# A gated transformer block on one core: attention output turned by whole transposes into two banks, six gate banks for the last batch, operands filled with zeros, new step lists

## What is computed

```python
x = x + tanh(g_xattn[0]) * L0_xattn(ln(x), ctx)   # auto-correlation attention by FFT, top 5 delays
x = x + tanh(g_ffn[0])   * L0_ffn(ln(x))          # product keys: 8 heads x 8 of 1024 experts
x = x + tanh(g_xattn[1]) * L1_xattn(ln(x), ctx)   # 16 heads of 8 channels, rotary positions
x = x + tanh(g_ffn[1])   * L1_ffn(ln(x))          # 8 experts of 336 hidden units, silu(gate) * up
```

## Time and profile before

| what | us |
|---|---|
| median of three runs (lowest, highest) | 447.41 (446.62, 448.52) |
| profiled execution, its own time | 448.5 |
| its span, first to last instruction | 446.6 |
| TensorE busy | 375.3 (84%) |
| VectorE busy | 324.0 (73%) |
| ScalarE busy | 197.5 (44%) |
| GpSimd busy | 103.6 (23%) |

### The profile page before, as it was taken

How to read it: one execution, slowest core, us unless ns; L and a number is a source line. 1 busy time by engine, 2 the same in 40 slices (tenths; PEclk the granted TensorE clock), 3 DMA queues, 4 the chain that set the end, 5 groups by cost and what they waited for, 6 DMA issues and landing times.

```text
span 446.6 us, 8078 instructions
## 1 busy us (share of the span) xinstructions
PE 375.3 (84%) x2848; PEld 291.4 (65%) x2848; DVE 324.0 (73%) x1255; ACT 197.5 (44%) x399; POOL 103.6 (23%) x221
## 2 busy tenths in 40 slices
...
GB/s 232 332 240 0 1 1 1 1 48 118 1 1 0 1 1 0 1 2 2 0 2 1 1 3 0 1 2 1 13 1 0 1 3 12 1 0 1 13 0 12
DMA packets 5773, 11.81 MB, mean 26 GB/s; under 512 B 2020, under 2 KB 4325, under 8 KB 5222
## 3 DMA queue, kind: packets, MB, share of 16 engines
...
...
## 4 chain that ended last, share of the span: by engine, by line
PE 36%; DVE 32%; issue 3%; ACT 2%; POOL 2%; DVEq 0%; ACTq 0%; POOLq 0%
PE ps L1192 35%; DVE Xb L1036 6%; DVE mx L1096 5%; DVE tix L937 2%; DVE HDb L1051 2%; DVE Y L1028 2%; DVE pk L946 1%; DVE Sb L1048 1%; DVE Xb L1048 1%; ACT L564 1%; DVE sb_downT L1018 1%; DVE hot L985 1%; DVE hot L983 1%; DVE sc L943 1%; DVE xnb L1156 1%
## 5 line engine op out<-in xcount | busy, mean ns | idle before, releaser
L1192 PEld LDWEIGHTS ps<-dnb,Sb 128*128 128x128 f32 x448 | 53.8, 192 | 7.8 <-issue 3.9
L1192 PE MATMUL ps<-dnb,Sb 128*128 128x128 f32 x448 | 56.4, 278 | 2.3 <-DVE xnb L1156 0.8
L1192 PE MATMUL ps<-Y,Xb 128*128 128x32 f16 x512 | 39.9, 251 | 16.3 <-DVE Xb L1036 10.1
L1192 PEld LDWEIGHTS ps<-Y,Xb 128*128 128x128 f16 x512 | 37.0, 163 | 22.1 <-DVE Xb L1036 16.8
L694 ACT ACTIVATE Sb<-ps 128x256 f32<-128x256 f32 x84 | 31.8, 382 | 37.4 <-PE ps L1192 37.3
L1192 PE MATMUL ps<-Xb,sb_guT 128*128 128x256 f32 x168 | 43.7, 390 | 1.8 <-DVE Sb L1166 1.2
L1156 DVE SCALAR_TENSOR_TENSOR xnb<-ps,score,xnb 128x128 f32<-128x128 f32 x56 | 17.0, 345 | 37.7 <-PE ps L1192 37.6
L1192 PE MATMUL ps<-ctxTb,sb_guT 128*128 128x256 f32 x168 | 44.2, 392 | 0.1
L1036 DVE TENSOR_TENSOR Xb<-sb_downT,iox 128x2048 f16<-128x2048 f16 x32 | 40.6, 1280 | 1.5 <-PE ps L1192 1.3
L471 ACT ACTIVATE Sb<-ps 128x256 f32<-128x256 f32 (+2 forms) x54 | 26.2, 493 | 34.4 <-PE ps L1192 19.5
L564 ACT ACT_TABLE_LOAD x32 | 41.1, 1283 | 0.6
...
## 6 DMA issues: line engine op xcount, KB each, us to landing
...
```

Of the source, the lines that this page charges most:

```text
L1192: return pe.matmul(o, l, r, start=start, stop=stop)
```

## The change

- **out_turn.** The attention output of four heads stands in a 128x256 block, each head in 32 rows of which 9 matter (8 channels and the sum). Before, eight products with a matrix that picks these 9 columns wrote 288 columns of bank 2. Now eight transposes of whole 128x128 blocks write 1024 columns, banks 2 and 3, and VectorE's attend reads them with a stride of 32. out_turn therefore claims bank 3 as well.
- **Banks for the last batch.** Gates of batches 0 to 2 alternate between banks 0 and 1 as before. The 21 gates of batch 3 go round six banks (0, 1, 4, 5, 6, 7) and wait for the previous gate in the same bank; on a bank from 4 up they wait until all prob steps are done. The downs of batch 3 alternate between banks 2 and 3.
- **Zero-filled operands.** The bias b_q is loaded as 128 rows (one of values, 127 of zeros) and multiplied with 128 rows of ones; the actor's first weight has 128 columns instead of 50; its second has 128 rows instead of 51, with ah of 128 rows.
- **New lists** for all four engines. They hold the same steps. In TensorE's list five of the nine warm steps now stand among the first batch's tokens and all before out_turn0.0; score1.3 and down0.1 come before mix2.0; in VectorE's list number0.0 and groups0.0 come earlier, best3.1 after weigh1.7, where3.1 and pair3.1 later.

```diff
@@ lists, TensorE: before, then after
-onehots0.0 token0.0 token0.1 token0.2 token0.3 token0.4 token0.5 token0.6 token0.7 mix0.0 onehots1.0 warm0.0 turn_20.0
-query0.0 warm0.1 turn_q0.0 warm0.2 by_query0.0 warm0.3 token1.0 by_query0.1 warm0.4 token1.1 by_query0.2 token1.2
...
-value0.1 token1.7 score0.3 value0.2 mix1.0 value0.3 out_turn0.0 onehots2.0 warm0.7 attend0.0 project0.0 turn_21.0
...
-gate0.7 score1.0 down0.0 token2.6 score1.1 value1.0 token2.7 score1.2 value1.1 mix2.0 score1.3 down0.1 onehots3.0
...
-gate2.16 gate2.17 down2.5 gate2.18 turn_33.0 gate2.19 route13.0 gate2.20 gate3.0 down2.6 gate3.1 gate3.2 route23.0
-gate3.3 gate3.4 down2.7 gate3.5 down3.0 gate3.6 gate3.7 down3.1 gate3.8 gate3.9 gate3.10 down3.2 gate3.11 down3.3
-gate3.12 gate3.13 gate3.14 gate3.15 down3.4 gate3.16 gate3.17 gate3.18 down3.5 gate3.19 gate3.20 down3.6 down3.7
+onehots0.0 warm0.0 token0.0 token0.1 warm0.1 token0.2 token0.3 token0.4 warm0.2 token0.5 token0.6 token0.7 warm0.3
+warm0.4 mix0.0 turn_20.0 onehots1.0 query0.0 turn_q0.0 warm0.5 by_query0.0 by_query0.1 token1.0 token1.1 by_query0.2
...
+score0.2 value0.1 token1.7 value0.2 score0.3 mix1.0 value0.3 out_turn0.0 onehots2.0 attend0.0 turn_21.0 project0.0
...
+score1.1 gate0.7 token2.6 value1.0 score1.2 value1.1 token2.7 down0.1 score1.3 mix2.0 gate0.8 value1.2 onehots3.0
...
+gate0.14 by_query2.0 token3.1 down0.3 by_query2.1 gate0.15 gate0.16 down0.4 by_query2.2 token3.2 attend1.0 gate0.17
...
+gate2.17 down2.5 gate2.18 turn_33.0 gate2.19 gate2.20 route13.0 gate3.0 gate3.1 gate3.2 down2.6 gate3.3 gate3.4
+down2.7 gate3.5 route23.0 gate3.6 gate3.7 down3.0 gate3.8 gate3.9 gate3.10 down3.1 gate3.11 gate3.12 gate3.13 down3.2
+down3.3 gate3.14 gate3.15 gate3.16 gate3.17 down3.4 down3.5 gate3.18 gate3.19 gate3.20 down3.6 down3.7
@@ lists, VectorE: before, then after
-weigh1.3 place1.5 place1.6 weigh1.4 weight2.1 weigh1.5 place1.7 weigh1.6 best3.0 best3.1 weigh1.7 where3.0 norms11.0
-pair3.0 attend0.0 groups2.0 norms30.0 where3.1 rope1.0 place2.0 pair3.1 place2.1 weigh2.0 place2.2 max1.0 place2.3
+place1.5 weigh1.4 place1.6 place1.7 weigh1.5 weight2.1 weigh1.6 best3.0 weigh1.7 best3.1 where3.0 norms11.0 pair3.0
+attend0.0 groups2.0 norms30.0 rope1.0 place2.0 place2.1 where3.1 weigh2.0 max1.0 place2.2 place2.3 weigh2.1 max1.1
...
+times3.4 times3.5 times3.6 moe_out2.0 rank3.0 times3.7 times3.8 times3.9 gather3.0 times3.10 gather3.1 gather3.2
+gather3.3 times3.11 times3.12 times3.13 times3.14 times3.15 gather3.4 gather3.5 times3.16 times3.17 times3.18
@@ -291,7 +291,7 @@
         score = sb("score", [P, 2, 16])
-        ah = sb("ah", [64, 2 * P])
+        ah = sb("ah", [P, 2 * P])
...
         up = [Sb[:, 1024:1280], Sb[:, 1280:1536], Xb[:, 2816:3072]]
@@ -305,6 +305,19 @@
         G_BANK = [4 + n % 4 for n in range(2 * EH)]
+        ROOMY = 3 * NB
+        WIDE = (0, 1, 4, 5, 6, 7)
+        def GATE_BANK(m):
+            return m % 2 if m < ROOMY else WIDE[(m - ROOMY) % len(WIDE)]
+        def GATE_BEFORE(m):
+            return max((n for n in range(max(0, m - len(WIDE)), m) if GATE_BANK(n) == GATE_BANK(m)), default=None)
+        def DOWN_BANK(b, e):
+            return 2 + e % 2 if b == 3 else 2
...
         DIRECT = (2, 3)
@@ -688,10 +701,10 @@
                 if b not in DIRECT:
-                    copy(up[m % 3], ps[:, m % 2, 256:512], "up_ready")
+                    copy(up[m % 3], ps[:, GATE_BANK(m), 256:512], "up_ready")
...
                     act.wait_ge(sem("y3_psum"), (m - 6) // NB * E8 + users((m - 6) % NB) + 1)
-                act.activation(av[:, m % 6, :], ps[:, m % 2, 0:256], ACT.Silu).then_inc(sem("gate_ready"), 1)
+                act.activation(av[:, m % 6, :], ps[:, GATE_BANK(m), 0:256], ACT.Silu).then_inc(sem("gate_ready"), 1)
...
                       "prob": prob, "keep": keep, "attend": attend, "route1": route1, "route2": route2,
@@ -1103,7 +1116,7 @@
                 v.wait_ge(sem("o_psum"), b + 1)
-                o = ps[:, 2, 0:288].rearrange("p (c d) -> p c d", d=9)
+                o = ps[:, 2:4, :].rearrange("p t (c w) -> p (t c) w", w=HW)
...
                                 rcp[:, :].unsqueeze(2).broadcast_to([P, 2 * H, DK]), ALU.mult).then_inc(sem("att_ready"), 1)
@@ -1148,7 +1161,7 @@
                 for t in range(2):
-                    y = ps[:, 2, t * D:t * D + D]
+                    y = ps[:, DOWN_BANK(b, e), t * D:t * D + D]
...
                         i = v.tensor_scalar(macc[:, t, :], y, w, None, ALU.mult)
@@ -1163,7 +1176,7 @@
                 v.wait_ge(sem("gate_ready"), m + 1)
-                v.tensor_tensor(av[:, m % 6, :], av[:, m % 6, :], ps[:, m % 2, 256:512], ALU.mult).then_inc(sem("av_ready"), 1)
+                v.tensor_tensor(av[:, m % 6, :], av[:, m % 6, :], ps[:, GATE_BANK(m), 256:512], ALU.mult).then_inc(sem("av_ready"), 1)
...
                 x4 = cur[:, 2 * b:2 * b + 2, :]
@@ -1424,7 +1437,7 @@
                     mm(o, xn2T[:, t * P:t * P + P], ld["Wq1"][:, :], True, False)
-                    i = mm(o, ones[0:1, 0:P], ld["bq1"][:, :], False, True)
+                    i = mm(o, ones[:, 0:P], ld["bq1"][:, :], False, True)
...
             def turned(signal):
@@ -1486,11 +1499,10 @@
                 claim(2, "att_ready", b + 1)
-                pick = ident[:, :].rearrange("p (r d) -> p r d", r=4)[:, :, 0:9]
+                claim(3, "att_ready", b + 1)
...
                     for g in range(4):
-                        o = (4 * t + g) * 36
-                        i = mm(ps[:, 2, o:o + 36].rearrange("p (r d) -> p r d", r=4), oT[:, g, t * P:t * P + P], pick)
+                        i = pe.transpose(ps[:, 2 + t, g * P:g * P + P], oT[:, g, t * P:t * P + P], ident[:, :])
...
             def attend(b, _):
@@ -1520,7 +1532,7 @@
                 claim(2, "ah_ready", b + 1)
-                mm(ps[0:AH, 2, 0:256], ld["w1T"][:, :], xn3T[b % 2]).then_inc(sem("ah_psum"), 1)
+                mm(ps[:, 2, 0:256], ld["w1T"][:, :], xn3T[b % 2]).then_inc(sem("ah_psum"), 1)
...
                 pe.wait_ge(sem("ah_ready"), b + 1)
@@ -1528,7 +1540,7 @@
                 for t in range(2):
-                    i = mm(ps[:, 2, 272 + t * MK:272 + t * MK + MK], ah[0:AH + 1, t * P:t * P + P], ld["w2T"][:, :])
+                    i = mm(ps[:, 2, 272 + t * MK:272 + t * MK + MK], ah[:, t * P:t * P + P], ld["w2T"][:, :])
...
             def gate(b, n):
@@ -1538,19 +1550,23 @@
                     pe.wait_ge(sem("xn3T_ready"), b + 1)
-                if m >= 2:
-                    pe.wait_ge(sem("av_ready" if (m - 2) // NB in DIRECT else "gate_ready"), m - 1)
+                held = GATE_BEFORE(m)
+                if held is not None:
+                    pe.wait_ge(sem("av_ready" if held // NB in DIRECT else "gate_ready"), held + 1)
+                if GATE_BANK(m) >= 4:
+                    pe.wait_ge(sem("p_ready"), 8 * B)
                 for s in range(2):
-                    i = mm(ps[:, m % 2, s * 256:s * 256 + 256], ld["guT"][:, s, n * P:n * P + P], xn3T[b % 2])
+                    i = mm(ps[:, GATE_BANK(m), s * 256:s * 256 + 256], ld["guT"][:, s, n * P:n * P + P], xn3T[b % 2])
...
                 pe.wait_ge(sem("av_ready"), b * NB + last(e) + 1)
-                claim(2, "y3_used", m + 1)
+                bank = DOWN_BANK(b, e)
+                claim(bank, "y3_used", m + 1)
...
                     for n in range(first(e), last(e) + 1):
-                        i = mm(ps[:, 2, t * D:t * D + D], av[:, (b * NB + n) % 6, t * P:t * P + P],
+                        i = mm(ps[:, bank, t * D:t * D + D], av[:, (b * NB + n) % 6, t * P:t * P + P],
@@ -1606,6 +1622,11 @@
+    def padded(x, rows=P, columns=None):
+        r = np.zeros((rows, columns or x.shape[1]), np.float32)
+        r[:x.shape[0], :x.shape[1]] = x
+        return r
@@ -1616,7 +1637,7 @@
         "rows": np.concatenate([i["L0_xattn_bq"], i["L0_xattn_bk"], i["L0_xattn_bv"], i["L1_xattn_b_kv"][:P]])[None],
-        "bq1": i["L1_xattn_b_q"][None], "bo1": i["L1_xattn_b_o"][None],
+        "bq1": padded(i["L1_xattn_b_q"][None]), "bo1": i["L1_xattn_b_o"][None],
...
         "w_q": i["L0_ffn_w_q"], "w_qT": i["L0_ffn_w_q"].reshape(D, 16, P).transpose(2, 1, 0),
@@ -1624,8 +1645,8 @@
         "Wq1": i["L1_xattn_W_q"], "Wkv1": i["L1_xattn_W_kv"], "Wo1": i["L1_xattn_W_o"],
-        "rw": i["L1_ffn_router_w"].T, "w1T": i["L1_ffn_actor_w1"].T, "b1": i["L1_ffn_actor_b1"][:, None],
-        "w2T": np.concatenate([i["L1_ffn_actor_w2"].T, i["L1_ffn_actor_b2"][None]], 0),
+        "rw": i["L1_ffn_router_w"].T, "w1T": padded(i["L1_ffn_actor_w1"].T, P, P), "b1": i["L1_ffn_actor_b1"][:, None],
+        "w2T": padded(np.concatenate([i["L1_ffn_actor_w2"].T, i["L1_ffn_actor_b2"][None]], 0)),
```

More of the change, by code:

```diff
@@ L72 @@
[L72 to L75, removed]
-gate1.18 gate1.19 score3.0 down1.5 gate1.20 down1.6 gate2.0 route12.0 gate2.1 route22.0 score3.1 down1.7 gate2.2
@@ new lines @@
+score1.1 gate0.7 token2.6 value1.0 score1.2 value1.1 token2.7 down0.1 score1.3 mix2.0 gate0.8 value1.2 onehots3.0
```

(20 more changed lines are left out.)

74 lines of the change are left out of this document (33 added, 41 removed).

## The result

The changed kernel takes 437.09 us, the median of four runs (435.98 to 437.86), against 447.97 us for the kernel before (four runs): a ratio of 0.976 with a 95% interval of 0.972 to 0.979. The forecast was 437.4 in a range of 432.0 to 443.5. The size is right; its working is not right in every term, and that two misses cancel is luck.

What follows compares the result with a forecast made beforehand. VectorE was taken to bound the kernel up to about 248 us (mix2.0), TensorE after. Terms -0.2 - 2.85 - 2.5 - 1.6 - 0.4 - 3.6 = -11.15, with 1.2 given back -10.0: 438.5 profiled, 437.4 us median, range 432.0 to 443.5.

Steps and rivals of the forecast that it cites:

- Before mix2.0: VectorE's waits ahead of mix2.0: 1.38 us for mix1.0 covered, a new 1.15 us before groups2.0; sum -0.2 us.
- Fit is close: TensorE's slack before mix2.0, a 1.01 us wait and shorter ones, was to cover the 2.85 us of moved work.
- the warm-up steps and the rest of the reshuffling I cannot price by a row: List changes ahead of mix2.0, bounded at -1.4 to +2 us and taken at none.
- Moved work: score1.3 (1.07 us) and down0.1 (1.78 us) go ahead of mix2.0: -2.85 us after it, 0 without cover.
- out_turn, -2.5: Eight whole transposes replace sixteen instructions: -0.83 us each, three of four behind the handover at mix2.0, -2.5 us.
- query, -1.6: Bias filled to 128 rows removes the change between one and 128 rows: -0.79 us each, query2.0 and query3.0, -1.6 us.
- The tail: From gate3.0 to TensorE's last matmul, six gate banks and alternating down banks cut 5.1 us of waits to 1.5: -3.6 us.
- Given back: Waits for already late engines, like value3.3's for ScalarE's copy, grow as TensorE arrives earlier: 0 to 3 us, taken +1.2.
- (1): VectorE takes over until mix3.0, so 4.6 us saved after mix2.0 is waited away: about 441 us; chance 0.17.
- (2): Padding leaves query as it is, or ScalarE and VectorE hold the last batch's gates: 439.4 to 441 us; chance 0.08.
- (3): out_turn's transposes don't overlap, 0.30 us each, 2.4 us per out_turn: 4.6 us lost, 442.0 us; chance 0.02.
- (4): Moved warm steps lengthen TensorE's idle at 200 to 220 us; low clock lasting to 248 gives 451 us; chance 0.05.

Runs made afterwards that it cites:

- a3: Changed kernel with warm0.7 put back behind onehots2.0 and warm0.8 behind query1.0 in TensorE's list; 437.77 us, ratio 0.977 to the kernel before.
- a6: Changed kernel with new lists and six banks, but the old out_turn and unfilled operands; 441.32 us, ratio 0.985 to the kernel before.
- a1: Changed kernel with the old out_turn (36-column products into bank 2, no claim on bank 3); 438.11 us, ratio 0.979 to the kernel before.
- e5: Kernel before with the six banks, and route13.0 moved behind gate2.20 (TensorE) and silu2.20 (ScalarE) in its old lists; 445.57 us, ratio 0.995.
- a4: Changed kernel with only the first batch's out_turn writing banks 0 and 1; 436.77 us, ratio 0.974 to the kernel before.
- b1: Changed kernel, first batch's out_turn in banks 0 and 1, warm0.7 behind attend0.0, warm0.8 behind query1.0; 435.85 us, ratio 0.974 to the kernel before.
- e1: Kernel before, old lists, with out_turn as eight whole transposes and its claim on bank 3; 446.71 us, ratio 0.996.
- e2: Kernel before, old lists, with bq1, w1T, w2T and ah filled with zeros to 128 rows and columns; 447.65 us, ratio 0.999.
- e6: Kernel before with all three code edits, and route13.0 moved behind gate2.20 (TensorE) and silu2.20 (ScalarE) in its old lists; 443.23 us, ratio 0.990.
- e3: Kernel before, old lists, with six banks for the last batch's gates and two for its downs; 449.50 us, ratio 1.002.
- e4: Kernel before, old lists, with all three code edits (transposes, filled operands, six banks); 448.01 us, ratio 0.999.

## Why the prediction was right, and where it was not

**Against the profiled execution** the forecast was -10.0 us; it became 448.5 - 437.86 = -10.6.

**Before mix2.0: forecast -0.2, measured +1.8** (248.36 to 250.14). The two waits were there: the one for mix1.0 shrank by 0.9, and the one before groups2.0 is 1.29. Two steps failed. The first is "Fit is close": the moved work was to be covered by TensorE's slack, and the cover was 1.1 us short, since score1.3 ends 1.14 us after VectorE's last weigh, where mix2.0 used to follow it at 0.06. The second is "the warm-up steps and the rest of the reshuffling I cannot price by a row", taken at none: VectorE's chain ends 0.7 us later instead of 0.2 earlier.

Counted from mix1.0 to mix2.0 the stage grew by 5.4 us. Of these 3.2 are waits of VectorE and 2.2 are its work: 1.1 of the work is what it does behind weigh2.7 while TensorE finishes score1.3, and 0.9 is the part of best3.1 that now lies behind the start of mix1.0, so that covering the wait moved work rather than saved it. Of the three later waits the one of 1.49 falls to 0.33 in a3, where the claim stays and the clock is higher; the one of 0.75 is also in a6, which has no claim; a1 has only one, of 0.69. So none is shown to be the claim's alone, and how it adds the rest is not shown. The larger loss is partly hidden by an earlier start: the first onehots0.0 is at 99.69 before and 95.75 after. One best step (1.5 us, half of the 3.07 in the earlier trace rows) explains part of that, since number0.0 now precedes best1.0; the rest is no effect of the change, for e5, with before's lists there, has it at 97.04. Positions ahead of mix2.0 therefore carry an uncertainty of over 2 us from one execution; distances behind it don't (181.9 in the changed kernel, a3, a4 and b1).

**Behind mix2.0: forecast -9.75, measured 194.6 to 181.9, -12.7.** Term by term:
- Moved work, -2.85: as forecast, 249.06 + 1.08 - 247.11 = 3.03 us of it stand ahead of mix2.0 now. 1.1 of it was not free there, as said above, so the move gained about 2 us.
- out_turn, -2.5: three take 2.73 us instead of 5.18, -2.45. e1 gave 1.6 us alone. The wait for rope2.0 that the forecast had seen and taken at nothing is 0.41 us in e1 and 0.40 in the changed kernel (out_turn1.0 at 265.68).
- query, -1.6: two take 1.78 instead of 3.22, -1.44. Filling the row does take the cost away, as the cause named would have it; no run separates the change between one row and 128 rows from the one-row product itself. e2 shows that the saving is waited away under the old lists.
- route1, -0.4: the two matmuls take 0.50 to 0.53 in batches 1 and 2 against 0.57, so about -0.05 each; the forecast of 0.14 each was nearly three times too large.
- The tail, -3.6: gate3.0 to the end is 35.1 us instead of 39.8, -4.7, and so 0.4 above the 34.7 that the forecast counted as work; it had left 1.5 of waits. The wait forecast before gate3.0 is there, with 0.44 in the row; the one at down3.2 is not.
- Given back, +1.2: it did not happen. value3.3 waits 0.6 us for ScalarE's copy in both kernels. The step "such waits grow as TensorE gets there earlier" failed: the new lists moved the steps of ScalarE and VectorE along, as e2 against the changed kernel shows at value2.3.
- Not in the sum: the gates behind mix2.0 take 70.1 us instead of 73.5, by the starts of the 76 gates and of the steps after them, and 1.7 of this is in the tail already (20.2 to 18.5). This comes with the new lists: the other kernels that have them, all with the six banks, need 69.7 to 70.2, and e1 to e6, with six banks or without, 73.7 to 79.1. 29 of the 76 are followed by another gate instead of 18, and a gate behind a down needs 0.87 instead of 0.96 (medians). Which of these features of the lists does it was not tried.

So a miss of 2.0 us before mix2.0 and one of 3.0 behind it, of opposite signs, left 1.0 at TensorE's end and 0.6 in the execution's time. That they cancel is luck.

**The rivals.** (1) VectorE did not take over until mix3.0: mix2.0 to mix3.0 fell from 58.1 to 52.8, and VectorE has 10 of 52.9 us free. (2) The forms did get cheaper. In e3 and e4 its second half was true all the same: with the old lists the last batch is held by ScalarE whatever the banks, and one place undoes it. (3) Eight transposes take 0.90 to 0.93 us, so they overlap. The rule of the Trainium skill, "TensorE: Matmul & The Clock Gate", Part 4, of about 275 ns each, does not give the pace here; it agrees with the recorded length of a single one, 277 ns on the mean of out_turn's 24 in batches 1 to 3. (4) The clock did fall further, to 0.61 from 200 to 220 us, and is 0.98 from there to mix2.0, so the low level did not last as this rival needed. It was not free: with two warm steps put back (a3) the clock is 0.74, VectorE's wait at 222 us 0.33 instead of 1.49, and the stage from mix1.0 to mix2.0 1.1 us shorter. The time shows no gain from it, a ratio of 0.977 against 0.976. Under the old lists e1 has a clock of 0.57 there and no such wait.

**What the argument missed as a whole** is that it priced the edits one by one and took the lists as the place where moved work stands. Edits without lists are worth nothing that can be measured (e4), edits with one place 4.6 us, with the whole lists 10.8.
